# Choosing a routed layer's experts in groups of batches, with the output indices computed beside the scatters

## What is computed

```python
def _L0_ffn_ref(x, Wg, W1, W2, W3, Ws1, Ws2, Ws3):   # TOP_K = 4, E = 32 experts, H = 128
    scores = jax.nn.softmax(xf @ Wg, axis=-1)
    weights, indices = jax.lax.top_k(scores, TOP_K)
    ...
    for e in range(E):
        pos = jnp.nonzero(pair_expert == e, size=C, fill_value=P)[0]
        ...
        out = swiglu(xg, W1[e], W2[e], W3[e]) * w[:, None]
        y = y.at[tok].add(out)
    z = swiglu(xf, Ws1, Ws2, Ws3)
    return (y + z).reshape(B, S, D)
```

## Time and profile before

| | us |
|---|---|
| median of 3 runs (lowest, highest) | 2698.16 (2696.84, 2705.11) |
| the profiled execution, its own time | 2706.32 |
| its span | 2704.3 |
| busy in the span: TensorE, VectorE, ScalarE, GpSimd | 2299.8, 1270.6, 848.1, 866.2 |
| granted TensorE clock, mean of the span | 0.921 |
| scatters of the block, 128 of them, GpSimd busy | 124.9 |

### The profile page before, as it was taken

How to read it: one execution, slowest core, us unless ns; L and a number is a source line. 1 busy time by engine, 2 the same in 40 slices (tenths; PEclk the granted TensorE clock), 3 DMA queues, 4 the chain that set the end, 5 groups by cost and what they waited for, 6 DMA issues and landing times. The chain is left out here.

```text
span 2704.3 us, 39994 instructions
## 1 busy us (share of the span) xinstructions
PE 2299.8 (85%) x12186; PEld 1627.9 (60%) x12187; DVE 1270.6 (47%) x2717; ACT 848.1 (31%) x1915; POOL 866.2 (32%) x1109
## 2 busy tenths in 40 slices
PE   6998856673999926698888887999999999999998
PEld 3454834442777722243333333655589999999998
DVE  5554135344444446677677765379322222222222
ACT  2222202220444403455565565322212222222221
POOL 2000003563000043654344121122235444445544
PEclk9999656886999967899899999999999999999999
DMA  9993116222555543544334220410047777777775
GB/s 338 372 365 133 58 28 249 86 95 81 157 156 156 152 125 83 106 111 101 71 73 102 67 72 13 162 39 16 16 139 245 246 245 245 246 249 247 247 246 168
DMA packets 246074, 412.60 MB, mean 153 GB/s; under 512 B 29958, under 2 KB 223855, under 8 KB 237784
## 3 DMA queue, kind: packets, MB, share of 16 engines
q1 hardware_dynamic: 206040, 351.70, 38.4%
q0 software_dynamic: 39936, 59.70, 10.7%
HBM read 261.83 MB, written 148.89 MB: 152 GB/s over the span
## 5 line engine op out<-in xcount | busy, mean ns | idle before, releaser
L2544 PE MATMUL me_hp<-me_xgT,me_w 128*128 128x160 f32 x3072 | 440.2, 300 | 0.6 <-DVE me_xgT L2586 0.6
L2544 PEld LDWEIGHTS me_hp<-me_xgT,me_w 128*128 128x128 f32 x3072 | 424.6, 191 | 1.5 <-DVE me_xgT L2586 0.7
L1349 DVE TENSOR_REDUCE hd_nmax<-hd_wide 128x2 f32<-128x1024 f32 x256 | 307.7, 1219 | 128.5 <-PE hd_wide L1094 124.3
L1278 ACT ACTIVATE hd_prob<-hd_slim 128x512 f32<-128x512 f32 x512 | 276.2, 601 | 190.4 <-PE hd_slim L1105 157.6
L2600 DVE TENSOR_TENSOR me_hid<-me_act_out,me_hp 128x160 f32<-128x160 f32 x384 | 123.5, 322 | 371.8 <-ACT me_act_out L2572 354.2
L1105 PE MATMUL hd_slim<-hd_q_stack,hd_k_stack 100*128 100x512 bf16 x512 | 199.9, 394 | 43.1 <-ACT hd_prob L1278 32.8
L2553 PE MATMUL me_op<-me_hid,me_w 128*128 128x160 f32 x1536 | 235.9, 303 | 0.0
L1094 PE MATMUL hd_wide<-hd_k_stack,hd_q_stack 97*128 97x512 bf16 x512 | 201.3, 398 | 29.5 <-DVE hd_rest L1343 15.9
L2572 ACT ACTIVATE me_act_out<-me_hp 128x160 f32<-128x160 f32 x384 | 116.8, 304 | 346.0 <-PE me_hp L2544 346.0
L2553 PEld LDWEIGHTS me_op<-me_hid,me_w 128*128 128x128 f32 x1536 | 213.7, 190 | 2.6
L1105 PEld LDWEIGHTS hd_slim<-hd_q_stack,hd_k_stack 100*128 100x128 bf16 x512 | 50.2, 99 | 197.7 <-ACT hd_prob L1278 84.7
(11 more groups left out here) (384 smaller groups left out, 3731.2 us busy)
## 6 DMA issues: line engine op xcount, KB each, us to landing
me_w<-in_L_ffn_w_exp SPq DMA_DIRECT2D x64, 2304.0 KB
places<-z_zero SPq DMA_DIRECT2D x64, 1152.0 KB, 11.2
mr_e_xt<-places SPq DMA_DIRECT2D x160, 144.0 KB, 2.2
outputs<-mr_e_y SPq DMA_DIRECT2D x160, 128.0 KB, 1.7
part_rows<-hd_parts SPq DMA_DIRECT2D x48, 256.0 KB
hd_k_stack<-part_rows SPq DMA_DIRECT2D x192, 64.0 KB
hd_q_stack<-part_rows SPq DMA_DIRECT2D x192, 64.0 KB
mr_w<-in_L_ffn_w_in SPq DMA_DIRECT2D x4, 2048.0 KB
```

Source lines behind the costliest of these rows:

```text
L1278: nc.scalar.activation(prob[:, u, :], slim[:, slim_slot(bt, item), :], ACT.Exp, scale=D ** -0.5)\
L1349: nc.vector.tensor_reduce(nmax[:, g % 2, n // 2, c:c + 2], wide[:, at], AX.X, ALU.max, negate=True)\
L2544: last = nc.tensor.matmul(hp[:, f % 3, half * CAP:(half + 1) * CAP], w1[:, sl, c, cols], xgT[:, sl, c, :], start=(c == 0), stop=(c == DC - 1))
```

## The change

The eight batches are chosen in three groups: batches 0 and 1, batches 2 to 4, batches 5 to 7. For a group, the logits of all its tiles lie side by side, and softmax, choice and places are single operations over 8 or 12 tiles (except `max` and `match_replace`, which stay one for a tile). The chained additions over tiles are gone: `ranking` sums over tiles in TensorE, by accumulating ones x `chosen` shifted by one tile, two tiles and so on, and ones x `carry`, the marks of the groups before. GpSimd waits for places once a group, so it issues 32, 48 and 48 scatters in a row. `xg` has six slots and `xT` five in place of four and two. The turned rows and the shared network's sums now share two PSUM buffers (`ring`), used in the order of a list. The Silu has a wait more (on `h_free`), the product too. The table is made before `add(4)`, and the output indices in four parts between the adds and products of the last batches. The semaphore clears stand before the loads of the experts' weights.

```diff
+            GROUPS = ((0, 1), (2, 3, 4), (5, 6, 7))
+            SLOTS, TURNED = 6, 5
...
+                    earlier.clear(sp)
                     for n in range(0, E, 8):
                         sp.dma_start(w1[:, n:n + 8]...)
...
-                    earlier.clear(sp)
...
-                    for b in range(B):
-                        pool.wait_ge(placed, b + 1)
-                        for j in range(TB):
-                            for n in range(TOP):
+                    for g in range(len(GROUPS)):
+                        pool.wait_ge(placed, g + 1)
+                        for b in GROUPS[g]:
+                            for j in range(TB):
+                                for n in range(TOP):
...
+                    def ranking(g):
+                        _, n = tiles_of(g)
+                        pe.wait_ge(sel_ready, g + 1)
+                        if g:
+                            pe.wait_ge(ranked, g)
+                        nc.tensor.matmul(ranks[:, 0:n, :], ones[:], carry[:].unsqueeze(1).to_broadcast([P, n, E]), start=True, stop=False)
+                        for d in range(1, n):
+                            nc.tensor.matmul(ranks[:, d:n, :], ones[:], chosen[:, 0:n - d, :], start=False, stop=False)
+                        nc.tensor.matmul(ranks[:, 0:n, :], tri[:], chosen[:, 0:n, :], start=False, stop=True).then_inc(rank_full, 1)
...
+                    turn(0)
+                    turn(1)
+                    logits(0)
+                    turn(2)
+                    first(0)
+                    ranking(0)
+                    turn(3)
+                    turn(4)
+                    logits(1)
+                    second(0)
+                    first(1)
+                    ranking(1)
+                    second(1)
+                    first(2)
+                    for b in (5, 6, 7):
+                        turn(b)
+                    logits(2)
+                    second(2)
+                    first(3)
+                    ranking(2)
+                    pe.wait_ge(counted, 1)
+                    nc.tensor.matmul(counts, ones[:], carry[:], start=True, stop=True).then_inc(lp_full, 1)
+                    second(3)
+                    for b in range(4, B):
+                        first(b)
+                        second(b)
...
-                        for j in range(TB):
-                            chain.link(nc.vector.tensor_tensor(before[:, j + 1, :], before[:, j, :], chosen[:, j, :], ALU.add))
...
+                    exponents(0)
+                    rows(2)
+                    choice(0)
+                    rows(3)
+                    placing(0)
+                    rows(4)
+                    hiddens(0)
+                    exponents(1)
+                    add(0)
+                    choice(1)
+                    hiddens(1)
+                    placing(1)
+                    add(1)
+                    rows(5)
+                    rows(6)
+                    hiddens(2)
+                    rows(7)
+                    exponents(2)
+                    add(2)
+                    choice(2)
+                    hiddens(3)
+                    placing(2)
+                    dve.sem_inc(counted, 1)
+                    add(3)
+                    hiddens(4)
+                    table_of_tiles()
+                    add(4)
+                    hiddens(5)
+                    shifts()
+                    add(5)
+                    hiddens(6)
+                    places_of_outputs(0)
+                    places_of_outputs(1)
+                    add(6)
+                    hiddens(7)
+                    places_of_outputs(2)
+                    places_of_outputs(3)
+                    add(7)
```

More of the change, by code:

```diff
@@ new lines, in mix_experts_routed, with ring_use @@
+            counted, tabled = s.sem("counted"), s.sem("tabled")
+            scattered = [s.sem(f"scattered{n}") for n in range(SLOTS)]
+            RING = [("turn", b, c) for b in range(5) for c in range(DC)] + [("sum", b, m) for b in (0, 1) for m in range(2)]\
+                + [("turn", b, c) for b in (5, 6, 7) for c in range(DC)] + [("sum", b, m) for b in range(2, B) for m in range(2)] + [("table",)]
+            def ring_use(item):
+                return RING.index(item), RING.index(item) % 2
@@ L1694, in first @@
-                    def first(b, n, half):
-                        if b and half == 0:
-                            pe.wait_ge(h_free, (b - 1) * NS + n + 1)
-                        for c in range(DC):
-                            last = nc.tensor.matmul(hp[:, n, half, :], sw1[:, n, c, half * F:(half + 1) * F], xT[:, b % 2, c, :],
-                                                    start=(c == 0), stop=(c == DC - 1))
-                        if half:
-                            last.then_inc(h_full, 1)
@@ new lines, in first @@
+                    def first(b):
+                        for n in range(NS):
+                            if b:
+                                pe.wait_ge(h_free, (b - 1) * NS + n + 1)
+                            for half in range(2):
+                                for c in range(DC):
+                                    last = nc.tensor.matmul(hp[:, n, half, :], sw1[:, n, c, half * F:(half + 1) * F], xT[:, b % TURNED, c, :],
+                                                            start=(c == 0), stop=(c == DC - 1))
+                            last.then_inc(h_full, 1)
@@ L1721, in second @@
-                        last.then_inc(y_full, 1)
-                    for c in range(DC):
-                        turn(0, c)
+                        for m in range(2):
+                            use, at = ring_use(("sum", b, m))
+                            emptied(use - 2)
+                            for j in (2 * m, 2 * m + 1):
+                                for n in range(NS):
+                                    last = nc.tensor.matmul(ring[:, at, (j % 2) * D:(j % 2 + 1) * D],
+                                                            hid[:, n, j * P:(j + 1) * P], sw2[:, n, :], start=(n == 0), stop=(n == NS - 1))
+                            last.then_inc(ring_full, 1)
@@ L1827, in hiddens @@
+                        chain.link(nc.vector.tensor_tensor(carry[:], carry[:], added[:], ALU.add))
                     def hiddens(b):
@@ new lines, in _ @@
+                    add(4)
[10 more added lines that the diff above has]
+                    add(7)
+                    use, at = ring_use(("table",))
+                    dve.wait_ge(ring_full, use + 1)
@@ L2626, in program @@
         x_loaded = [k.sem(f"x_loaded{n}") for n in range(4)]
-        scattered = [k.sem(f"scattered{j}") for j in range(TB)]
         gathered = [k.sem(f"gathered{j}") for j in range(TB)]
```

300 lines of the change are left out of this document (151 added, 149 removed).

## The result

The changed kernel takes **2755.28 us** (median of 4 runs, 2750.47 to 2759.04) against 2700.26 us for the kernel before in the same comparison: a ratio of 1.0204, 95% interval 1.0181 to 1.0227. It is 55 us slower, where 35 were forecast, inside the range. The profiled execution took 2750.47 us with a span of 2748.5.

What follows compares the result with a forecast made beforehand. TensorE's completions, late during uninterrupted scatter series, were taken to bound the first layer's routed experts stage. First scatter +13, gaps +13 and tail +9 gave +35 us: 2733 on the median, own range 2712 to 2762, full range down to 2664.

Steps and rivals of the forecast that it cites:

- The reading of the bound: First layer's routed experts before their loop: while scatters are issued, TensorE's completions arrive late, in order, after a prompt start-up.
- 3 us after the end: After an uninterrupted series of scatters: all late TensorE completions are taken to be forgiven 3 us after it ends.
- a budget of 80 instructions and then one per 0.7 us: TensorE completions per uninterrupted scatter series: some 80 instructions arrive at once, then one per 0.7 us.
- Rival A: Late arrivals come from other work, not a budget; scatters run unbroken, -36 us, 2662; chance 0.22.
- Rival B: Start-up longer in time than in instructions, or arrivals at 0.5 us; gaps 8 and 12, -6 us, 2692; chance 0.13.
- Rival C: Change does not do what it says; only clears ahead of the weights could be slow, priced at nothing; no chance given.
- First scatter: Start of the stage: first group's larger work delays the first scatter from 441.2 to 454.5 us, +13.
- Gaps: Between the three scatter series: gaps of 19 and 25 us, 44 where 31.1 were, +13.
- After the last scatter: Last batches' products remain after the flush; first load 32 us after the last scatter instead of 23.4, +9.
- the bound of 27: Upper bound of the term behind the last scatter: first load 50 us after it, +27.
- VectorE beside scatters: Indices' passes and row copies now run beside scatters; the trace showed no cost, so the sum holds nothing.
- The estimate of 9 us for the four parts: By the skill's rule, eight compare and multiply index passes would push scatters 9 us later, 2742; not adopted.

Runs made afterwards that it cites:

- a_paced: Changed kernel plus fourteen chained GpSimd memsets (some 5 us) between two batches of a group, five pauses: 2697.22 us, 0.9984 of the kernel before.
- b_pauses: Kernel before with clears first, output indices ahead of the last add, nine chained GpSimd memsets (some 3.3 us) between any two batches: 2688.21 us, ratio 0.9921.
- b_first_split4: Kernel before with each matmul of the shared experts' first product cut into four parts of 128 columns: 2699.97 us, ratio 0.9962.
- b_pauses_parts: b_pauses with the output indices in four parts of 1056 elements: 2686.47 us, ratio 0.9903 to the kernel before.
- a_clears_late: Changed kernel with the 56 semaphore clears moved back behind the expert weights' loads on SyncE's queue: 2756.37 us, ratio 1.0197 to the kernel before.

## Why the prediction was right, and where its sizes were off

**The reading of the bound held.** That completions are late in an unbroken series of scatters and arrive when it is over was read from the earlier trace rows and shown by a_paced: nothing but time without scatters was added, and gaps and tail fell. b_pauses shows it from the other side, in the kernel before. "3 us after the end" fits only series of 16 scatters. The prediction's own rows had 3.2 and 4.75 us behind 32, and behind the 48 of series 2 and 3 it was 6.7 and 6.4 us. What did not hold is the form of the law: a budget of 80 instructions and then one per 0.7 us is contradicted by b_first_split4, where 175 instructions had ended after 16.5 us. Rival A had unbroken scatters from 455 to 618; there were three series. Rival B's gaps of 8 and 12 us did not come either; its premise, a prompt start that is long in time rather than in instructions, does not fit all rows by itself, as the budget does not. Rival C, the clears, was priced at nothing and is nothing in the time.

**First scatter, +13 forecast, 9.7 measured.** The sum had +17 for a low clock and +9 for a full one; the clock was 0.75 in this stretch against 0.63 before, and the term came out near its lower end.

**Gaps, +13 forecast, 16.3 measured.** Gaps of 19 and 25 us were forecast, 22.2 and 25.3 came. That the sums of batch 0 and the logits of group 2 wait for the end of their series was placed rightly. Two errors inside hardly show. Group 1's logits were to be 25 us late, near 485, and were 6.7 us late, at 468.37; the sums that stand behind them in VectorE's order came at 492.91 all the same. And that group 2's logits were forecast for 578.7 and used at 578.79 is luck: the series ended 3.6 us earlier than forecast (572.06 for 575.7), and the results came 6.7 us after its end where 3 were taken.

**After the last scatter, +9 forecast, 23.4 measured**, within the bound of 27. This is the term that was mis-sized. It took one completion per 0.7 us, from the kernel before's series of 16 and 32 scatters, to hold through 48 of them, so that 150 of some 256 instructions got through and 105 remained. In the longer series they came more slowly: at the end of series 2 TensorE was down to a matmul and its load every 2.80 us, 1.4 us each, and in series 3 some 32 instructions lie between the arrivals of 628.65 and 665.13, 1.1 us each. TensorE posted its last work of series 3 at 623.65 and had 160 instructions left after it. Those 55 more, at the tail's 30.2 us for 160, are 10 us. The late last completion (6.4 us after the last scatter where 3 was taken) is 3.4 us more, and the rest, about 1 us, is small change.

**VectorE beside scatters, forecast at nothing.** In the changed kernel it cost nothing, though not for the reason given: the indices ran from 680.9 on, after the last scatter, and its scatters kept 0.97 us. I had set a 0.23 us copy against a rule of the Trainium skill, "SBUF — State Buffer", section "SBUF: two separate sides", and had applied what it says of a copy on both shared ports to compare and multiply passes. The same section names passes like these as a second case: a VectorE operation with two inputs in SBUF takes the shared pair for its whole length, and locks out a GpSimd operation that reads SBUF. In b_pauses the trace agrees, and it has a price: two scatters of 5.12 and 4.28 us beside compare and multiply passes of 4.56, which have two inputs, against 0.97 beside the reduction, which has one. A short copy was no row from which to dismiss it. The estimate of 9 us for the four parts could not be seen in the changed kernel, and in b_pauses_parts eight such passes cost some 1.4 us.

**An inference that does not follow.** The prediction took the near agreement of the median with the profiled execution as leaving no room for late arrivals that are the profiler's alone. All executions here, of either kernel, were recorded with their span and clock, so that comparison cannot tell.

**What the change had right** is its last part. Indices ahead of the last scatter's end take the tail from 23.4 to 6.9 us, and cut in four they hold the scatters up by some 0.4 us each; both pay once the completions come in time.

## What to carry to other kernels

Where GpSimd issues indirect DMAs back to back, look how long after a matmul's end its result is first used. If this grows within a series and vanishes a few us after it, longer series only move work behind their end. A break of some 3 us after every 16 scatters, fixed and not a wait that may already be met, gave back more than it cost here; behind 32 scatters 3.9 us were too short and 5.4 us were enough. Price a rate at the length at which it will be used: one that was measured in short series was 1.6 to 2 times too good for a long one.

## What the hardware did that was not expected

- A pause of GpSimd that does no useful work (25.6 us in all) shortened the kernel by 58 us. Pauses of 2.7 us in the kernel before made it 1.1% faster together with the earlier indices.
- In a long series TensorE's pace settles at one matmul per 2.80 us with nothing to wait for in the view. I have no cause for it. It is not the scatters' own data that is behind: in every series of the two kernels the last of its packets ended some 1.1 us after the last scatter was issued. None of the runs tells whether the lateness would be there without the recording that all of them had; nor was it tried whether fewer bytes for each scatter change it.
- Semaphore clears on SyncE that took 36 us beside scatters and weight loads (451.2 to 487.2 in the kernel before) took at most 3.7 us ahead of them (419.4 to 423.1), and neither place is seen in the time. In the kernel before they started 0.7 or 1.4 us apart, and the last five went through at 487, the moment at which VectorE used the held logits (487.08), so TensorE is not the only engine that is held. In a_clears_late, where they began together with the scatters, the same 56 took 8.2 us (447.8 to 455.9).
